# A gated attention and feed-forward layer: x tiles dealt once, their sums formed after the turn

## What is computed

```python
x = x + tanh(g_xattn) * attention(layernorm(x), ctx)      # 16 heads, RMS-normed q and k
h = layernorm(x)                                            # 4096 rows of 512
u = square(relu(h @ up_w))                                  # 512 -> 2048
y = u @ down_w + (h @ expert_weight) * (sum of the top two of h @ gate_w)
x = x + tanh(g_ffn) * (layernorm(y) * ln_gamma + ln_beta)
```

## Time and profile before

| | |
|---|---|
| median of 3 runs | 1452.31 us (1451.91 to 1452.99) |
| the profiled execution's own time | 1458.65 us |
| its span, first to last instruction | 1456.9 us |
| busy: TensorE, VectorE, ScalarE, GpSimd | 89%, 65%, 52%, 43% |
| mean granted TensorE clock | 0.942 |
| moved by DMA | 289.56 MB, 199 GB/s; 283772 of 388453 packets under 512 B |
| DMA queues, share of 16 engines | SyncE's (q1) 47.1%, ScalarE's (q10) 22.8% |

### The profile page before, as it was taken

How to read it: one execution, slowest core, us unless ns; L and a number is a source line. 1 busy time by engine, 2 the same in 40 slices (tenths; PEclk the granted TensorE clock), 3 DMA queues, 4 the chain that set the end, 5 groups by cost and what they waited for, 6 DMA issues and landing times.

```text
span 1456.9 us, 26472 instructions
## 1 busy us (share of the span) xinstructions
PE 1299.7 (89%) x9154; PEld 1107.7 (76%) x9154; DVE 947.3 (65%) x1540; ACT 757.5 (52%) x2012; POOL 629.4 (43%) x769
## 2 busy tenths in 40 slices
PE   7999999998999999978999958799968799998990
PEld 5877777777787787756999746699847699877990
DVE  5776776776778766555686545587546487465675
ACT  5876776776777676543453422453423454443440
POOL 3666666666669963544132422122423024120033
PEclk9999999999999999988999979899979899998996
DMA  6588888888898655478776677676677576563841
GB/s 211 146 217 218 215 219 213 216 222 206 217 228 196 164 117 188 148 228 222 269 247 201 216 189 159 217 244 208 204 207 186 205 232 199 205 232 105 236 144 58
DMA packets 388453, 289.56 MB, mean 199 GB/s; under 512 B 283772, under 2 KB 298236, under 8 KB 383231
## 3 DMA queue, kind: packets, MB, share of 16 engines
q1 hardware_dynamic: 350856, 178.90, 47.1%
q10 hardware_dynamic: 37494, 109.33, 22.8%
HBM read 205.08 MB, written 83.10 MB: 198 GB/s over the span
## 4 chain that ended last, share of the span: by engine, by line
PE 45%; DMA 14%; SPq 13%; issue 9%; POOL 8%; DVE 5%; ACT 2%; DVEq 0%; POOLq 0%; ACTq 0%
PE wide L79 14%; PE wide L80 13%; PE wide L81 13%; DMA pair<-x_scratch 5%; SPq L1630 4%; SPq L279 3%; DMA kd_scratch<-kf 3%; DMA k_dealt<-kd_scratch 3%; PE wide L418 2%; SPq L1182 1%; DMA fxy<-in_up 1%; PE wide L406 1%; POOL frstd L1441 1%; DMA out_x<-fxy 1%; ACT prob L817 1%
## 5 line engine op out<-in xcount | busy, mean ns | idle before, releaser
L817 ACT ACTIVATE prob<-wide,nmx 128x128 f32<-128x128 f32 x512 | 180.1, 392 | 5.2 <-DVE nmx L626 5.2
L988 POOL TENSOR_TENSOR prob<-prob,rr 128x512 f32<-128x512 f32 x128 | 136.3, 1079 | 76.5 <-DVE rr L634 76.3
L81 PE MATMUL wide<-eight,wo_lo 128*128 128x256 f32 x512 | 144.9, 283 | 0.0
L79 PE MATMUL wide<-eight,wo_hi 128*128 128x256 f32 x512 | 144.9, 283 | 0.0
L80 PE MATMUL wide<-eight,wo_hi 128*128 128x256 f32 x512 | 144.9, 283 | 0.0
L1980 DVE TENSOR_TENSOR wo_lo<-hid,wo_hi 128x512 fp32r<-128x512 f32 x128 | 101.5, 805 | 63.9 <-ACT wo_hi L1802 61.2
L1802 ACT ACTIVATE hid<-wide 128x512 f32<-128x512 f32 x96 | 57.2, 598 | 163.5 <-PE wide L81 163.5
L2128 POOL TENSOR_TENSOR pair<-pair,beta 128x512 f32<-128x512 f32 x24 | 32.1, 1340 | 242.8 <-DMA pair<-x_scratch 242.8
L817 ACT ACTIVATION_READ_ACCUMULATOR prob<-wide,nmx 128x1 f32 x512 | 119.5, 233 | 0.0
L1802 ACT ACTIVATE wo_hi<-hid 128x512 fp32r<-128x512 f32 x128 | 79.6, 632 | 73.0 <-PE wide L81 73.0
L79 PE MATMUL wide<-wq_hi,eight 128*128 128x512 f32 x192 | 84.9, 442 | 28.8 <-DVE eight L565 26.9
(11 more groups left out here) (276 smaller groups left out, 4100.8 us busy)
## 6 DMA issues: line engine op xcount, KB each, us to landing
eight<-down_scratch ACTq DMA_DIRECT2D x32, 1024.0 KB, 6.6
xn_scratch<-xs SPq DMA_DIRECT2D x48, 256.0 KB, 6.0
wk_hi<-down_scratch ACTq DMA_DIRECT2D x12, 1024.0 KB, 5.9
wk_lo<-down_scratch ACTq DMA_DIRECT2D x12, 1024.0 KB, 7.2
hid<-xn_scratch SPq DMA_DIRECT2D x48, 256.0 KB, 4.8
wk_hi<-up_scratch ACTq DMA_DIRECT2D x12, 1024.0 KB, 8.6
eight<-up_scratch ACTq DMA_DIRECT2D x12, 1024.0 KB, 7.2
wk_lo<-up_scratch ACTq DMA_DIRECT2D x12, 768.0 KB, 5.1
```

The lines of the kernel that those rows point to most:

```text
L79: eng.matmul(dst, ah, bh, start=first and k == 0, stop=False, skip_group_check=onto)
L81: mm = eng.matmul(dst, al, bh, start=False, stop=last and k == n - 1, skip_group_check=onto)
L817: i = act.activation(prob[par][:, g, h * P:(h + 1) * P], cols(bank[g], h), ACT.Exp, bias=nmx[:, n:n + 1], scale=1.0, accum_out=rs[:, n:n + 1])
L988: pool.tensor_tensor(p, p, r, ALU.mult).then_inc(po_p, 1)
```

## The change

In groups 2 to 4 only the eight x tiles are dealt, fetched and turned. The four sums of a pair are formed by GpSimd on the turned tiles, in place (`turned_sums`), between its low parts; the turns stand at steps 9 to 17, the high parts at steps 11 to 20 (x tiles) and 31 to 45 (sums). All eight x tiles are loaded at q 0, dealt at q 4 and 5. Residual tiles have four buffers; the order of y's steps, stores and residual loads is new. The first group has four piece buffers. The experts start with half of two products on the first chunk. The last product of the last group runs block by block, and each block is collected by itself. In attention `unit_store` and `unit_hi_raw` move. The core of the diff:

```diff
@@ attention, SyncE: slot @@
                     if has(s + 4):
                         load(s + 4, par, t["x"], xin, ld_x)
+                    if ff.third_of(s, par) is not None:
+                        ff.unit_store(sp, ff.third_of(s, par))
                     if kq_dealt(n):
                         at_least(sp, dv_kf, n + 1, apart=True)
                         deal(sp, kf, kd_dram[1 - par], st_kd)
...
-                    if uu is not None:
-                        ff.unit_store(sp, uu)
-                        if not isinstance(uu, int) or uu + 2 < 2 * ff.NU:
-                            ff.unit_load(sp, uu + 2)
+                    if uu is not None and (not isinstance(uu, int) or uu + 2 < 2 * ff.NU):
+                        ff.unit_load(sp, uu + 2)
@@ attention, ScalarE: slot @@
-                    if ff.first_of(s, par) is not None:
-                        ff.unit_hi_raw(act, ff.first_of(s, par))
...
                     if has(n + 1):
                         hi_xT(n + 1)
+                    if ff.first_of(s, par) is not None:
+                        ff.unit_hi_raw(act, ff.first_of(s, par))
@@ first group, pieces @@
-        return flat(fxy[:, 2 * (w % 2):2 * (w % 2) + 2, :])
+        return flat(fxy[:, 2 * ((w - 2) % KT):2 * ((w - 2) % KT) + 2, :])
@@ the next group's operands @@
+            if i < GB:
+                act.wait_ge(dv_tr, (g - 1) * GB + i + 1)
+                act.wait_ge(pe_E, g * GB)
+            else:
+                act.wait_ge(po_ts, KT * ((g - 1) * HB + i % HB + 1))
...
+    def turned_sums(pool, g, jj):
+        (a0, a1), (b0, b1) = ([hid[i][:, 0, :].rearrange("p (c m) -> p c m", c=KT)[:, :, n * P // 2:(n + 1) * P // 2] for n in range(2)]
+                              for i in (jj, jj + HB))
+        n = KT * ((g - 1) * HB + jj)
+        pool.wait_ge(dv_tr, (g - 1) * GB + HB + jj + 1)
+        pool.wait_ge(po_lT, (g - 1) * NT + HB + jj + 1)
+        pool.tensor_tensor(a0, b0, a0, ALU.subtract).then_inc(po_ts, 1)
+        pool.tensor_tensor(b0, b1, b0, ALU.subtract).then_inc(po_ts, 1)
+        pool.wait_ge(po_ts, n + 2)
+        pool.tensor_tensor(b1, b1, a0, ALU.subtract).then_inc(po_ts, 1)
+        pool.wait_ge(po_ts, n + 3)
+        pool.tensor_tensor(a1, a1, b1, ALU.subtract).then_inc(po_ts, 1)
...
-    TURN_AT = (9, 12, 14, 16, 26, 29, 31, 33, 36, 38, 40, 42, 45, 47, 49, 52)
+    TURN_AT = (9, 10, 12, 13, 14, 15, 16, 17)
+    HI_AT = (11, 12, 14, 15, 16, 17, 18, 20, 31, 33, 35, 37, 39, 41, 43, 45)
@@ SyncE: group @@
+                    else:
+                        for i in range(HB):
+                            load_res(g - 1, i)
                     if more:
-                        load_x(g + 1, 0)
+                        load_x(g + 1)
+                if g == 0 and 0 < q < NQ - 1:
+                    ff.piece_store(sp, q + 1)
+                    if q + 5 < NQ + 2:
+                        ff.piece_load(sp, q + 5)
+                if g > 0 and q in (2, 5):
+                    for i in range(2 * (q // 5), 2 * (q // 5) + 2):
+                        store_out(sp, g - 1, i)
+                        load_res(g - 1, i + HB)
+                if more and q in (4, 5):
+                    for tile in range(HB * (q - 4), HB * (q - 3)):
+                        deal(g + 1, tile)
...
+                for i in range(HB, GB):
+                    store_out(sp, g - 1, i)
@@ TensorE: experts, last product @@
+            ff.chunk_ready(pe, g, 2 * NQ)
+            part(0, 0)
+            part(1, 0)
+            ff.upward(pe, g, NQ - 1, 4)
+            ff.chunk_ready(pe, g, 2 * NQ + 1)
...
+        def last_product(g):
...
+            for j in range(HB):
+                for q in range(NQ):
+                    if j == 0:
+                        pe.wait_ge(ff.dv_l, NK * g + NQ * m + q + 1)
+                    mm = down_part(g, m, q, j)
+                mm.then_inc(ff.pe_S, 1)
@@ ScalarE: group @@
+                if g > 0:
+                    ff.ring_load(act, g, 2 * q + 3)
                 copy_a6(g, q)
@@ VectorE: fill and end @@
+            if g > 0 and q in (2, 5):
+                for i in range(2 * (q // 5), 2 * (q // 5) + 2):
+                    result(g - 1, i)
+            if g < LAST:
+                for tile in {1: range(HB), 2: range(HB, GB)}.get(q, ()):
+                    ff.stats(dve, g + 1, tile)
+                for tile in {3: range(HB), 4: range(HB, GB)}.get(q, ()):
+                    ff.normalise(dve, g + 1, tile)
...
+            if i >= HB:
+                collect_last(LAST, i - HB)
             y_centre(LAST, i)
@@ GpSimd: group @@
                 for i in range(NT):
+                    if GB <= i < GB + HB:
+                        ff.turned_sums(pool, g + 1, i - GB)
                     ff.lo_T(pool, g + 1, i)
```

More of the change, by code:

```diff
@@ L1172, in second_of, with third_of @@
         return uu if par == 1 and (not isinstance(s, int) or 0 <= uu < 2 * NU) else None
+    def third_of(s, par):
+        uu = s - 4
+        return uu if par == 0 and (not isinstance(s, int) or 0 <= uu < 2 * NU) else None
     def quarters_of(a):
@@ L1602, in res, with split_slot @@
     def res(g, i):
-        return ff.last_res[:, i, :] if g == LAST else ff.pair[:, i % 2, :]
+        return ff.last_res[:, i, :] if g == LAST else (ff.pair if i % HB < 2 else ff.sums)[:, i % 2, :]
     def turn_in(i):
-        return hid[i % HB][:, 0, :]
+        return (ff.sums if i % HB < 2 else ff.pair)[:, i % 2, :]
+    def split_slot(g, k):
+        if g == LAST and k >= NK - NQ:
+            a, n = (ff.xa, ff.ta)[(k - (NK - NQ)) // HB], k % HB
+            return a[0][:, n, :], a[1][:, n, :]
+        return ff.s_hi[k % HB], ff.s_lo[k % HB]
@@ L1664, in group @@
+            sp.dma_start(res(g, i), ff.dealt_rows(x2_dram[g * GB + i])).then_inc(ff.ld_r[i % HB], DMA)
         def group(g):
@@ L1712, in _ @@
             group(g)
-        for i in range(GB):
-            store_out(LAST, i)
+        for i in (0, 1, 2, 3, 4, 6):
+            store_out(sp, LAST, i)
         for n in range(HB):
@@ L1795, in _ @@
             experts(g)
-            for k in range(NK):
+            for k in range(NK if g < LAST else NK - NQ):
                 downward(g, k)
+            if g == LAST:
+                last_product(g)
     @block.scalar
@@ L1850, in split_hi @@
             if k == 0 and g < LAST:
-                for s in range(GB):
-                    act.wait_ge(ff.st_n[s], 2 * (g + 1) * DMA)
-            at_least(act, ff.pe_S, NK * g + k - KT + 1)
+                act.wait_ge(ff.st_n, GB * (g + 1) * DMA)
+            if g == LAST and k >= NK - NQ:
+                act.wait_ge(ff.dv_l, NK * g + 2 * NQ)
+                act.wait_ge(ff.pe_E, GB * NG8)
+            else:
+                at_least(act, ff.pe_S, NK * g + k - KT + 1)
             if m in (0, 5):
@@ L2039, in y_centre @@
             centre(g, i)
-        def fill_a(g, q):
-            if g > 0:
-                for i in {2: (0, 1), 6: (4,)}.get(q, ()):
-                    result(g - 1, i)
-            if q == 5:
-                routing(g)
         def fill_b(g, q):
@@ L2083, in group @@
             if g > 0:
-                result(g - 1, 5)
-                result(g - 1, 6)
-                y_centre(g - 1, 7)
+                for i in range(HB, GB):
+                    result(g - 1, i)
             sum_3(g, NQ - 1)
@@ L2089, in group @@
                 sums_21(g, q)
-                if q == HB and g > 0:
-                    result(g - 1, 7)
             for k in range(NK):
```

376 lines of the change are left out of this document (154 added, 222 removed).

## The result

The changed kernel takes 1381.24 us (1377.95 to 1385.71, 4 runs) against 1452.65 (1451.91 to 1453.51, 4 runs): a ratio of 0.951, 95% interval 0.948 to 0.954. Beside the experiments it was run again, unaltered, and took 1384.70 (1380.63 to 1386.96) against 1450.81, ratio 0.954 (0.951 to 0.958). The forecast was 1384, within 1357 to 1419.

The account below looks back on a forecast made before the run. Waste was put in U, E, tail and attention, with loads queued behind SyncE's deals; -32.6-38-20+18+7-7 = -72.6, less 5 given back, -68: 1390.7 us profiled, 1384 median; own range 1368 to 1400, overall 1357 to 1419.

Parts of the forecast that it names:

- no deal stands ahead of a load that VectorE's statistics await: Groups 2 to 4, up products: U takes 84 us in the second and third, -32.6 together.
- eight deals in a row occupied that queue for 33.8 us: SyncE's queue before; the four-engines rival took this as all groups 2 and 3 partly win back, 14 us each.
- The sums in D: GpSimd's sums join a chain in three D stages; 5 us of stall and 1 for clock each: +18, bounds 0 and +30.
- The link: In D, one high part, one low part and four sums: 5.7 us, where ScalarE gives two steps, 2.9 us.
- the eight turns stand within a step of 1.44 and the lead hides them: In D, each turn is one VectorE and one ScalarE instruction; uncovered they cost about 1 us.
- the exclusion that I had as a rival for the sums alone: In D, VectorE's 0.69 us instruction before each GpSimd sum: +25; within the longer-chain rival, chance 0.13.
- k's deal stands behind the whole store: Attention: k's load about 1 us later in some nine pairs, less what early x gives: +7, bounds -57 and +27.
- The 5 us given back: Taken off the summed gain of 72.6 us for what turns late next, stores in E and ring loads: -68.
- a bound by the four engines in U: Rival: four DMA engines still bound U and E; groups 2 and 3 gain 14 us each, 1415 us; chance 0.18.
- attention freed: Rival: only x's chain was late and k is carried along; attention -25 in place of +7, 1352 us; chance 0.14.
- the longer chain in D: Rival: chain in D longer by exclusion or clock, +21 more, 1405 us; chance 0.13.
- the slower case: Rival: GpSimd's sums in D take 2.8 us each, 68 us more; at 3.2 us a sum 1467 us; chance 0.05.

Follow-up runs that it names:

- sixteen deals: Changed kernel with each of the eight x tiles dealt a second time at q 6 and 7, into scratch nobody reads: 1411.28 us.
- the sums ahead: Changed kernel with GpSimd's sums of all four pairs ahead of its low part 8, not one pair ahead of each low part 8 to 11: 1373.96 us.
- the move alone: Kernel before with only the attention part of the change (unit's store and raw high parts moved): 1455.56 us against 1452.21, ratio 1.0035.

## Why the prediction was right, and which of its steps were not

The main mechanism held: with no deals ahead of the loads, U runs from end to end and E is short. The one large step that failed is D.

**U and E.** The forecast for groups 2 to 4 was -70.6, the stages give -72.2. U came to 82.0, at the pace of the last group, where I took 84; E to 29.4, 28.3 and 23.6 against 27, 27 and 26. Some 4 us of the -72.2 may be the long profile of before, as said above. The step "no deal stands ahead of a load that VectorE's statistics await" held. The queue does make E: with sixteen deals E is long again. What failed is the size put on a deal, which the sum did not use and a rival did: "eight deals in a row occupied that queue for 33.8 us" was read as their cost, and it is 13.6. The rest of such a stretch is waiting. In the changed kernel four deals that follow two stores and two residual loads took 30.7 us; in the same time GpSimd's residual waited 20.8 us for the first of those loads and then 8.5 for the second. Whether those transfers on four engines are what the deals waited for is argued from this order alone; residual loads and stores spread over sixteen engines were not tried. It costs nothing in U, and in E at most what is over 22.3 us. In the second group's E, TensorE's own matmuls are part of that: busy 22.05 us at a mean granted clock of 0.87, against 19.36 at 1.00 in the first group's.

**First group.** -24.9 against -20, past the bound of -21. Cut as above U took 79.6 and E 22.1, where I had taken 81.9 and 24.6. The 24.5 of E was worked out from D's pace for 102 matmuls; cut as after, E has 96, and where TensorE does not wait it takes 22.1 to 22.3.

**The sums in D.** +29.7 against +18, within the bounds 0 and +30. The link was right: 5.7 forecast, 5.96 measured, and the stalls stood where forecast, though "about two a stage of 2 to 3 us" were one of 2.9 and one of 1.2, with D at 90.6 and not at 86 to 87. The term of the sum that was mis-sized is what lies beside it: "5 us of stall and 1 for the clock" a stage is 6.5 of idle and 3.4 by which TensorE was longer busy (84.05 us for what took 80.6). Of the 3.4, the clock is 1.7 (0.98 over the stage); with the sums ahead, at 1.00, 2.2 are left, so the rest goes with the waits and not with the clock. The step that failed is that the eight turns stand within a step of 1.44 and the lead hides them: a turn of 0.70 and a low part of 0.68 do fit in 1.44, a turn and a low part of 1.16 do not, and I left GpSimd's low parts beside them out of that step. That is the exclusion that I had as a rival for the sums alone, with +25 for it. The Trainium skill, "SBUF — State Buffer", section "Who interferes with whom", names it: a VectorE instruction with two SBUF inputs and a GpSimd one that reads SBUF exclude each other. This case's rows agree: 0.68 becomes 1.22 beside sums that take 0.73 alone, in alternation, while transposes keep their 0.70 and a collect out of PSUM its 1.21. By shares: the chain and GpSimd's place together cost 4.5 us a stage (90.6 to 86.1 with the sums on VectorE), the low parts beside the turns 1.9 more (84.2, in a run that also moved the sums to other steps), and 3.6 is left.

**Attention.** +7 against -3.6 between the profiles, which looks like an error of sign and is none. Undone, it gives 6 to 10 us, alone in the kernel before it costs 2 to 8. The step as put, "k's deal stands behind the whole store", is what the landing times show, 7.5 for 3.3 us; that x's deal is early shows too, 3.3 us in place of some 7. But the sum was 1 us in each of nine pairs, and about half of the cost is a tenth long slot that it did not count, so the size is in part luck. The last block of scores stood at 545.6 to 551.2 us in seven profiles with the changed attention (548.4 in the mean), at 536.3 to 542.2 in four of the changed kernel with the store's old place (540.0). In the kernel before it stood at 549.5 in the one profile with the old place, whose nine long slots add up to 180.0 us, and at 547.9 in the one with the move alone. So the -3.6 holds the shortest attention of seven against the one of before, which was longer than any of the four with the same order on the queue; why it was, no run shows.

**Tail.** -9.6 against -7, inside the bounds; the first output store stood at 1349.36, 5.4 us ahead of TensorE's end at 1354.76. **The 5 us given back** were found nowhere; they happened to cover a part of what D cost more.

So the total was near for a sound reason in the largest terms and by balance in the rest: D cost 12 us more than forecast, U, E, the first group and the tail gained 9 more, and the 5 given back were not taken.

Of the rivals: a bound by the four engines in U fell (U at 82.0); attention freed fell; the longer chain in D came true by half of its size (+12 of +21); the slower case needed sums of 2.8 us, and they took 0.73 to 1.2.

## What to carry to other kernels

Work moved from one engine's idle stretch into another stage keeps about its duration and changes its neighbours: cost it with what the shared neighbour does there, step by step, above all VectorE's two-input instructions beside GpSimd's. A queue's long stretch of issues isn't the price of those issues: before it is counted as a gain, ask how much of it is waiting for data or behind other transfers; doubling the issues measures it. And where two profiles disagree with the medians, look for the stage that varies from execution to execution, and undo the part on the chip before giving it a sign.

## What was unexpected

The two engines don't merely slow each other; they take turns. Beside sixteen sums, 0.73 us each where alone, twelve of VectorE's instructions of 0.68 us ran at 1.21 or 1.22, all alike. And moving a store later in its queue, away from the deal that it held up, cost 21 to 25 us where I expected at least 6 back: it made another engine wait for the buffer that it empties. The order on the queue had been good for two reasons, of which the profile of before showed one.
